# Three-pass scores from split keys, a bias kept in DRAM and half sums on GpSimd, in a two-layer cross-attention kernel

## The chip, the cores and the metric

The kernel runs on one core of a Trainium2 chip. The metric is device time in microseconds. A core has TensorE (PE; its weight loads are listed apart as PEld), VectorE (DVE), ScalarE (ACT), GpSimd (POOL) and SyncE (SP, which here only issues transfers). Each engine runs its own instructions in order; they wait for each other by semaphores. SBUF is the on-chip memory, PSUM the banks in which matrix products are added up.

## The reference

64 batches of 128 queries x 128 channels go through two layers. Each layer is a gated cross-attention with 16 heads of 64 over 77 keys (context rows of 128 channels), and a gated feed-forward part, on normalised x:

```
q, k, v = x @ Wq, context @ Wk, context @ Wv          # 16 heads of 64
sim  = einsum('bhid,bhjd->bhij', q, k) * 64 ** -0.5   # layer 1: masked keys get -max
attn = softmax(sim, axis=-1)
out  = einsum('bhij,bhjd->bhid', attn, v) -> (B, N, 1024) @ Wo + bo
x    = x + tanh(g) * out
```

The feed-forward part of layer 0 is a quantised GELU one, that of layer 1 a spiking one with five steps. The change leaves both alone.

## The kernel before

**Stages.** fold_weights (layer 0), attention (0), quantised_ffn, fold_weights (1), attention (1), spiking_ffn. Folding makes, per head, A = Wk^T Wq and B = Wv Wo as 128 x 128 matrices, and keeps each as a high half in f32r and a low half (`Ahi`, `Alo`, `Bhi`, `Blo`). So a head's "keys" are A times the context, and scores are one product of turned x with them.

**Attention.** 64 slots, one for each batch t, with a 65th to finish. Four batches are a group (b = t % 4 is the slot in its group), eight an octet. In slot t:
- keys for the next group: four heads a slot. A product is three f32r passes of 128 x 308 (hi.hi, lo.hi, hi.lo; make_keys, L512 to L514) into one of two PSUM banks pP; ScalarE copies it out (L656) to G, an f32 tile with two sides, one a group.
- values for the next octet: `PLAN` = 3,3,3,3,3,3,2,0 a slot, three passes of 512 columns (L523 to L525) into the same two banks; ScalarE copies them to a ring ST (L662), SyncE sends them to DRAM, and fetches them back a batch at a time (send, fetch).
- scores of batch t: three full-precision f32 products (`UNITS`: 6, 6 and 4 heads; L573) of XT and G into banks pS0 to pS2. VectorE takes row maxima (L810) and subtracts them into E (L820); ScalarE does the exponential in place (L696); VectorE sums over the 77 keys (L854) and takes the reciprocal (L856); GpSimd multiplies in three parts (L898) into PN.
- batch t-1: TensorE turns PN in ten chunks (turn_probs, L593), ScalarE copies them (L705), TensorE multiplies with the fetched values (weigh, L608) into pO; VectorE adds the result to x (residual, L829) in slot t+1 of the program.
- once a group, for later ones: statistics (b=0, L744 to L752), normalise (b=1, L758), turn_x and its copy (b=2, L506, L652), statistics_after (b=2, L766 to L778; in layer 0 also row maxima and minima L769, L770), context turning and splitting (b=3, L99 to L113), and in layer 1 mask_bias (b=3, L738).

**Order.** It is written out by hand in each engine's `slot`. On TensorE: produce 0, 1, scores 0, produce 2, scores 1, (turn x or context), produce 3, scores 2, produce 4, turn_probs 0, produce 5, turn_probs 1, produce 6, weigh 0, turn_probs 2, weigh 1, weigh 2; keys and values alternate in `produce`. A product waits until ScalarE has copied out the one two before it. On VectorE: maximum 0, residual, shift 0, maximum and shift 1, (context low half), maximum and shift 2, then statistics, normalise, statistics_after or mask_bias, and last the sum and reciprocal.

**Mask, layer 1.** x is widened by a constant channel, so row 127 of G holds a bias per key. SyncE loads 308 mask bytes a group (load_mask, L439), VectorE makes 0 or -2^100 of them (mask_bias), and SyncE places that in four transfers (place_mask, L462). In slot b=3 mask_bias(group+2) waits for a load that SyncE issues at the top of its next slot, behind fetch(t+1).

## Time and profile before

Median of three runs 1606.85 us (1605.63 to 1610.71). The profiled execution took 1606.41 us, its span (first to last instruction) is 1604.8 us.

| | whole span | 300 to 400 us (layer 0) | 1000 to 1100 us (layer 1) |
|---|---|---|---|
| TensorE busy | 90% | 99.4 us | 95.3 us |
| VectorE busy | 68% | 69.9 | 62.5 |
| ScalarE busy | 56% | 65.0 | 60.6 |
| GpSimd busy | 39% | 37.5 | 38.2 |
| granted TensorE clock, of 2.4 GHz | 0.97 | 1.00 | 0.97 |
| DMA share | 36% | 46% | 43% |

A busy time is a share of a stretch, and the ends of matrix products in the records are modelled and overlap the next one's start; what one costs in a full stream is the step from its start to the next. Where an engine was idle ahead of an instruction, the timeline gives the idle time and the engine and line that ended it. "SPq" is SyncE's queue. The slots of the first attention end at about 624 us, those of the second run from about 837 to 1442 us.

### The profile page before, as it was taken

The numbers are of one execution on the slowest core, as the hardware profiler recorded it, in microseconds if no ns is written. First come the engines' busy times: TensorE is split into PE (matmuls) and PEld (weight loads), VectorE is DVE, ScalarE is ACT, GpSimd is POOL, SyncE is SP. The second block draws the span as 40 slices with busy tenths as digits, with TensorE's granted clock in tenths as the row PEclk, the third lists the DMA queues.
The fourth block names the chain that finished last, engine by engine and source line by source line (L and its number), as shares of the span: only waits on it lengthen the run. The fifth ranks groups of instructions, "written<-read, shape, count | busy, mean of one in ns | idle before, by whom it ended". The sixth has DMA issues, their size and how long they took to land. (4 is left out here: it accounts for less than half of the span.)

```text
span 1604.8 us, 27395 instructions
## 1 busy us (share of the span) xinstructions
PE 1447.1 (90%) x9094; PEld 1200.3 (75%) x9094; DVE 1089.5 (68%) x2356; ACT 903.2 (56%) x1903; POOL 624.0 (39%) x747
## 2 busy tenths in 40 slices
PE   6999999999999986559798999898999999977996
PEld 5888888888888874229777878787878787766884
DVE  5676676776777776898655757575656665773886
ACT  3666666666666653660155656565656565545662
POOL 1233434334334333840113333333334342445885
PEclk9999999999999999899999999999999999998998
DMA  8554444444444422100064444444444444320111
GB/s 253 178 157 134 141 153 131 159 130 154 136 151 130 146 80 69 30 0 0 18 192 136 131 139 132 131 130 133 133 135 133 134 128 134 100 64 1 33 33 40
DMA packets 198330, 182.27 MB, mean 114 GB/s; under 512 B 14145, under 2 KB 195393, under 8 KB 198209
## 3 DMA queue, kind: packets, MB, share of 16 engines
q1 hardware_dynamic: 197632, 180.60, 35.8%
q8 instruction: 67, 1.10, 0.3%
q14 instruction: 55, 0.44, 0.1%
q10 hardware_dynamic: 576, 0.13, 0.0%
HBM read 95.43 MB, written 84.93 MB: 112 GB/s over the span
## 5 line engine op out<-in xcount | busy, mean ns | idle before, releaser
L898 POOL TENSOR_TENSOR PN<-E,RC 128x512 f32<-128x512 f32 (+1 forms) x384 | 336.7, 906 | 584.7 <-DVE RC L856 583.7
L810 DVE TENSOR_REDUCE MX<-pS 128x6 f32<-128x462 f32 (+1 forms) x384 | 222.2, 579 | 260.2 <-PE pS L573 260.2
L608 PE MATMUL pO<-work,PT 128*128 128x128 f32 (+1 forms) x2560 | 331.7, 277 | 29.1 <-ACT PT L705 29.1
L656 ACT ACTIVATE G<-pP 128x308 f32<-128x308 f32 (+1 forms) x488 | 209.0, 429 | 244.3 <-PE pP L514 244.1
L608 PEld LDWEIGHTS pO<-work,PT 128*128 128x128 f32 (+1 forms) x2560 | 309.4, 192 | 37.3 <-issue 35.4
L573 PE MATMUL pS<-G,XT 128*128 128x462 f32 (+1 forms) x768 | 324.4, 507 | 0.0
L696 ACT ACTIVATE E<-E 128x462 f32<-128x462 f32 (+1 forms) x384 | 209.6, 546 | 152.5 <-DVE E L820 144.6
L512 PE MATMUL pP<-Chi,Ahi 128*128 128x308 f32 x496 | 240.5, 485 | 1.4 <-ACT G L656 1.2
L820 DVE TENSOR_TENSOR E<-pS,MX 128x462 f32<-128x462 f32 (+1 forms) x384 | 223.7, 582 | 9.1 <-issue 0.2
L705 ACT ACTIVATE PT<-pT 128x512 f32<-128x512 f32 (+1 forms) x384 | 201.0, 523 | 49.7 <-PE pT L593 49.7
L593 PE MATMUL pT<-ident,PN 128*128 128x128 f32 (+1 forms) x1280 | 202.6, 277 | 27.5 <-POOL PN L898 27.5
L854 DVE TENSOR_REDUCE SM<-E 128x16 f32<-128x1232 f32 x128 | 183.4, 1432 | 34.6 <-ACT E L696 34.1
L662 ACT ACTIVATE ST<-pP 128x512 f32<-128x512 f32 x290 | 172.1, 594 | 46.7 <-PE pP L525 41.5
L593 PEld LDWEIGHTS pT<-ident,PN 128*128 128x128 f32 (+1 forms) x1280 | 159.0, 141 | 48.9 <-issue 31.9
L523 PE MATMUL pP<-Bhi,Vhi 128*128 128x512 f32 x300 | 153.6, 512 | 12.1 <-PEq L145 9.3
L573 PEld LDWEIGHTS pS<-G,XT 128*128 128x128 f32 x768 | 136.2, 188 | 24.1 <-issue 6.4
L513 PE MATMUL pP<-Chi,Alo 128*128 128x308 f32 x496 | 151.3, 305 | 0.0
L514 PE MATMUL pP<-Clo,Ahi 128*128 128x308 f32 x496 | 151.1, 305 | 0.0
L512 PEld LDWEIGHTS pP<-Chi,Ahi 128*128 128x128 f32 x496 | 95.1, 192 | 35.3 <-issue 20.8
L524 PE MATMUL pP<-Blo,Vhi 128*128 128x512 f32 x300 | 121.0, 403 | 0.0
L525 PE MATMUL pP<-Bhi,Vlo 128*128 128x512 f32 x300 | 120.9, 403 | 0.0
L513 PEld LDWEIGHTS pP<-Chi,Alo 128*128 128x128 f32 x496 | 95.1, 192 | 32.2 <-issue 25.3
(194 smaller groups left out, 1960.3 us busy)
## 6 DMA issues: line engine op xcount, KB each, us to landing
values<-ST SPq DMA_DIRECT2D x256, 256.0 KB
work<-values SPq DMA_DIRECT2D x512, 128.0 KB
values<-ST SPq DMA_DIRECT2D x64, 208.0 KB
work<-values SPq DMA_DIRECT2D x128, 104.0 KB
C<-in_ctx SPq DMA_DIRECT2D x32, 154.0 KB
out<-s_O SPq DMA_DIRECT2D x16, 256.0 KB, 2.3
work<-in_L_xattn_Wq SPq DMA_DIRECT2D x2, 512.0 KB, 7.4
work<-in_L_xattn_Wkv SPq DMA_DIRECT2D x2, 512.0 KB, 7.8
```

What stands on the lines that cost most here:

```text
L512: nc.tensor.matmul(out, p["Ahi"][:, head, :], hi, start=True, stop=False)
L513: nc.tensor.matmul(out, p["Alo"][:, head, :], hi, start=False, stop=False)
L573: nc.tensor.matmul(out, XT[:, half, b, :], G[:, half, b, h0:h1, :].rearrange("p h k -> p (h k)"), start=True, stop=True).then_inc(score_re ...
L593: last = nc.tensor.transpose(pT[n % 2][0:rows, c - c0, :], PN[(t - 1) % 2][:, start:start + rows], p["ident"][:, :])
L608: last = nc.tensor.matmul(pO[:, 0:CH], PT[0:rows, c, :], V[(t - 1) % VRING][0:rows, tile, CH * hh:CH * hh + CH], start=c == 0, stop=c == C ...
L656: return nc.scalar.activation(G[0:live, g % 2, :, head, :], bank[0:live, 0:KEYCOLS].rearrange("p (b k) -> p b k", k=KEYS), ACT.Copy)
L696: nc.scalar.activation(e, e, ACT.Exp).then_inc(exp_done, 1)
L705: nc.scalar.activation(PT[0:rows, c0:c1, :], pT[n % 2][0:rows, 0:c1 - c0, :], ACT.Copy).then_inc(p_out, 1)
L810: nc.vector.tensor_reduce(MX[:, h0:h1], pS[u][:, 0:(h1 - h0) * KEYS].rearrange("p (h k) -> p h k", k=KEYS), X_AXIS, ALU.max).then_inc(max_ ...
L820: nc.vector.tensor_tensor(E[t % 2][:, h0:h1, :], pS[u][:, 0:(h1 - h0) * KEYS].rearrange("p (h k) -> p h k", k=KEYS), MX[:, h0:h1].unsqueez ...
L854: nc.vector.tensor_reduce(SM[:, :], E[t % 2][:, :, :], X_AXIS, ALU.add).then_inc(sum_done, 1)
L898: nc.gpsimd.tensor_tensor(out, e, scale, ALU.mult).then_inc(prob_ready, 1)
```

## The change

- Scores: x and keys are both kept as high and low f32r halves, and a score product is three passes of 308 columns (x_hi.k_hi, x_hi.k_lo, x_lo.k_hi), four of them a slot (`UNITS` is now four units of 4 heads), in three banks that are used in turn.
- Keys: instead of G with two sides there are Ghi and Glo with one 4 x 4 grid of cells each. Slot b of a group uses up a row of cells and refills it with the next group's keys; the next group reads them the other way round. A keys product is now copied out twice: ScalarE writes the high half, then VectorE the low half (`keys_lo`), and the bank is free after that.
- Order: values stand ahead of keys. VectorE does residual, statistics, normalise and statistics_after ahead of the first maximum, and the four low halves at the slot's end, with the total between the third and the fourth.
- Sum: E gets a 78th column of zeros; GpSimd adds columns 0 to 38 to columns 39 to 77 (into PN, which is free then), and VectorE reduces 16 x 39 instead of 16 x 77.
- Mask: in fold_weights of layer 1 all 64 x 77 mask bytes are loaded and turned into a bias, four heads wide, which goes to DRAM. In attention SyncE places a row of four cells a slot from there. The mask_bias of each group is gone. GpSimd zeroes Glo's last rows at the start.
- sem_clear moves from the second attention to the quantised feed-forward part.

```
-UNITS = [(0, 6), (6, 12), (12, 16)]
+UNITS = [(4 * u, 4 * u + 4) for u in range(4)]
+SCORES = len(UNITS)
+HALF = KEYPAD // 2
...
-            out = []
-            for j in range(4):
-                out += keys[j:j + 1] + values[j:j + 1]
-            return out
+            return values + keys
...
+        def cell(tile, g, b, quarter):
+            return tile[:, b, quarter, :] if g % 2 == 0 else tile[:, quarter, b, :]
...
# SyncE, slot t, between the sends and fetch(t + 1)
+                if layer == 1 and group + 1 < GROUPS:
+                    sp.wait_ge(score_ready, SCORES * (t + 1))
+                    place_bias(group + 1, t % GROUP)
...
# TensorE, produce
                         wait(pe, made_out, m - 1)
+                        if m >= 2 and KINDS[m - 2] == "key":
+                            pe.wait_ge(lo_out, keys_to(m - 1))
...
# TensorE, scores
+                    wait(pe, shifted, n - 2)
+                    out = pS[n % 3][:, 0:4 * KEYS]
+                    hi, lo = cell(Ghi, group, b, u), cell(Glo, group, b, u)
+                    nc.tensor.matmul(out, XThi[:, half, b, :], hi, start=True, stop=False)
+                    nc.tensor.matmul(out, XThi[:, half, b, :], lo, start=False, stop=False)
+                    nc.tensor.matmul(out, XTlo[:, half, b, :], hi, start=False, stop=True).then_inc(score_ready, 1)
...
# TensorE, order of slot t (v values, K0 to K3 keys): S0 V0 S1 V1 (turn) S2 V2 S3 K0
#   turn_probs0 K1 turn_probs1 K2 weigh0 turn_probs2 K3 weigh1 weigh2; with no values K0 is ahead of S3
...
# ScalarE, produced
                         if kind == "key":
-                            keys_out(pP[m % 2], group + 1, which).then_inc(made_out, 1)
+                            act.wait_ge(score_ready, SCORES * (t + 1))
+                            keys_hi(pP[m % 2], group + 1, which).then_inc(made_out, 1)
...
# ScalarE, order: V0 exp0 V1 (x_hi or context_hi) exp1 V2 K0 exp2 probs0 K1 exp3 probs1 K2 probs2 K3
...
# VectorE
+                def low(j):
+                    if values + j < len(todo):
+                        m = MADE[t] + values + j
+                        dve.wait_ge(made_out, m + 1)
+                        keys_lo(pP[m % 2], group + 1, todo[values + j][1]).then_inc(lo_out, 1)
+
+                def total():
+                    if cur:
+                        dve.wait_ge(half_done, t + 1)
+                        nc.vector.tensor_reduce(SM[:, :], PN[t % 2][:, 0:HEADS * HALF].rearrange("p (h k) -> p h k", k=HALF),
+                                                X_AXIS, ALU.add).then_inc(sum_done, 1)
...
                 if t >= 2:
                     residual(t - 2)
...
                 if b == 2 and t >= GROUP and cur:
                     dve.wait_ge(x_done, group * GROUP)
                     statistics_after(group - 1)
+                row_max(0)
+                shift(0)
+                row_max(1)
+                shift(1)
+                if b == 2 and nxt:
+                    x_lo(group + 1)
...
+                row_max(2)
+                shift(2)
+                row_max(3)
+                shift(3)
+                low(0)
+                low(1)
+                low(2)
+                total()
+                low(3)
...
# GpSimd
+            def halves(t):
+                pool.wait_ge(exp_done, SCORES * (t + 1))
+                wait(pool, p_turned, (t - 1) * 3)
+                nc.gpsimd.tensor_tensor(PN[t % 2][:, 0:HEADS * HALF].rearrange("p (h k) -> p h k", k=HALF),
+                                        E[t % 2][:, :, 0:HALF], E[t % 2][:, :, HALF:KEYPAD], ALU.add).then_inc(half_done, 1)
```

## Rows read from the trace of the kernel before

**Rows 1.** Timeline of TensorE, layer 0: start us, us, engine, line, operation, tiles.
```profile
303.99 0.60 PE L593 MATMUL pT<-ident,PN 128*128 128x128 f32 x4
...
304.71 0.30 PE L514 MATMUL pP<-Clo,Ahi 128*128 128x308 f32 x1
304.86 1.05 PE L608 MATMUL pO<-work,PT 128*128 128x128 f32 x8
305.75 0.38 PE L593 MATMUL pT<-ident,PN 128*104 128x128 f32 x2
...
307.45 0.30 PE L513 MATMUL pP<-Chi,Alo 128*128 128x308 f32 x1
...
308.20 0.39 PE L525 MATMUL pP<-Bhi,Vlo 128*128 128x512 f32 x1
308.43 0.94 PE L573 MATMUL pS<-G,XT 128*128 128x462 f32 x2
...
309.34 0.30 PE L513 MATMUL pP<-Chi,Alo 128*128 128x308 f32 x1
```

**Rows 2.** Timeline of VectorE: reciprocals of slots 30, 54, 58; 74 and 114 (layer 1).
```profile
335.42 0.25 DVE L856 RECIPROCAL RC<-SM 128x16 f32<-128x16 f32 x1
...
554.66 0.25 DVE L856 RECIPROCAL RC<-SM 128x16 f32<-128x16 f32 x1
...
588.03 0.25 DVE L856 RECIPROCAL RC<-SM 128x16 f32<-128x16 f32 x1
...
933.17 0.25 DVE L856 RECIPROCAL RC<-SM 128x16 f32<-128x16 f32 x1
...
1329.30 0.25 DVE L856 RECIPROCAL RC<-SM 128x16 f32<-128x16 f32 x1
```

**Rows 3.** Timeline of VectorE, layer 0: slots with b=0 (309 us) and b=2 (328 us).
```profile
309.40 0.64 DVE L810 TENSOR_REDUCE MX<-pS 128x6 f32<-128x462 f32 x1 [2.51 <-PE pS L573]
...
312.88 0.86 DVE L744 BATCH_NORM_STATS2 BN<-X 128x6 f32<-128x128 f32 x4
...
314.36 1.44 DVE L854 TENSOR_REDUCE SM<-E 128x16 f32<-128x1232 f32 x1
...
328.30 0.34 DVE L829 SCALAR_TENSOR_TENSOR X<-pO,gate,X 128x128 f32<-128x128 f32 x1
328.55 0.63 DVE L820 TENSOR_TENSOR E<-pS,MX 128x462 f32<-128x462 f32 x1
...
330.60 0.48 DVE L810 TENSOR_REDUCE MX<-pS 128x4 f32<-128x308 f32 x1 [0.20 <-PE pS L573]
331.12 0.48 DVE L820 TENSOR_TENSOR E<-pS,MX 128x308 f32<-128x308 f32 x1
331.51 0.86 DVE L766 BATCH_NORM_STATS2 BN<-X 128x6 f32<-128x128 f32 x4
...
333.95 1.43 DVE L854 TENSOR_REDUCE SM<-E 128x16 f32<-128x1232 f32 x1
```

**Rows 4.** Timeline of TensorE and VectorE, start of attention 1 and its slots 18 to 20.
```profile
811.29 0.50 PE L523 MATMUL pS<-Bhi,Vhi 128*128 128x512 f32 x1 [2.27 <-ACT ST L662]
...
1008.50 0.86 DVE L766 BATCH_NORM_STATS2 BN<-X 128x6 f32<-128x128 f32 x4
...
1010.13 1.44 DVE L854 TENSOR_REDUCE SM<-E 128x16 f32<-128x1232 f32 x1
...
1027.43 0.31 DVE L738 TENSOR_SCALAR MB<-M 1x308 f32<-1x308 uint8 x1 [9.12 <-DMA M<-in_mask_BxS_bf]
...
1030.67 1.09 PE L593 MATMUL pT<-ident,PN 128*128 128x128 f32 x4 [4.01 <-POOL PN L898]
```

**Rows 5.** Groups by line and form: xcount, busy us, mean ns of one, idle time before.
```profile
L898 POOL TENSOR_TENSOR PN<-E,RC 128x512 f32<-128x512 f32 x256 | 271.4, 1082 | 584.7 <-DVE RC L856 583.7 <-PE pT L593 1.0
...
L883 POOL TENSOR_TENSOR X<-X,gbias 128x512 f32<-128x512 f32 x32 | 40.8, 1275 | 2.5 <-DVE XN L758 2.5
L652 ACT ACTIVATE XT<-pO 128x512 f32<-128x512 f32 x32 | 18.6, 581 | 0.6 <-PE pO L506 0.5
```

More of the change, by code:

```diff
@@ L178, in _ @@
                 load_weights(sp, p, w, loaded)
+            if layer == 1:
+                sp.dma_start(M8[:, :], w["mask"].rearrange("o (b k) -> (o b) k", k=KEYS)).then_inc(m_in, 16)
             sp.wait_ge(padded, CTX)
@@ L316, in _ @@
             if layer == 1:
+                dve.wait_ge(m_in, 16)
+                nc.vector.tensor_scalar(MB[:, :, :], M8[:, :].unsqueeze(1).to_broadcast([BATCH, 4, KEYS]), MASKED, -MASKED,
+                                        ALU.mult, ALU.add).then_inc(bias_made, 1)
                 dve.wait_ge(loaded["q"], 16)
@@ L348, in tile_rows, with attention @@
     return 128 if t < TILES - 1 else PAIR * TAIL
-def attention(nc, p, layer, ctx, ctx_dram, mask_dram):
+def attention(nc, p, layer, ctx, ctx_dram):
     with ExitStack() as s:
@@ L421, in products @@
             values = [("value", start + j) for j in range(PLAN[n])] if octet < OCTETS else []
-            out = []
-            for j in range(4):
-                out += keys[j:j + 1] + values[j:j + 1]
-            return out
+            return values + keys
+        KINDS = [kind for t in range(BATCH) for kind, _ in products(t)]
         MADE = [0]
@@ L612, in weigh @@
                         last.then_inc(out_ready, 1)
-                produce(0)
-                produce(1)
+                values = sum(1 for kind, _ in todo if kind == "value")
                 scores(0)
-                produce(2)
+                if values > 0:
+                    produce(0)
                 scores(1)
+                if values > 1:
+                    produce(1)
                 if b == 2 and nxt:
@@ L625, in slot @@
                     turn_context(nc, p, ctx, pO, group + CTX)
-                produce(3)
                 scores(2)
-                produce(4)
+                if values > 2:
+                    produce(2)
+                if values == 0:
+                    produce(0)
+                scores(3)
+                if values > 0:
+                    produce(values)
                 turn_probs(0)
-                produce(5)
+                produce(values + 1)
                 turn_probs(1)
-                produce(6)
+                produce(values + 2)
                 if prev:
                     if b == 2 and nxt:
-                        pe.wait_ge(xt_out, group + 2)
+                        pe.wait_ge(xhi_out, group + 2)
+                        pe.wait_ge(xlo_out, group + 2)
                     if b == 3 and cur and group + CTX < GROUPS:
@@ L640, in slot @@
                 turn_probs(2)
+                produce(values + 3)
                 weigh(1)
@@ L706, in probs_out @@
                                              ACT.Copy).then_inc(p_out, 1)
-                produced(0)
-                produced(1)
-                produced(2)
+                values = sum(1 for kind, _ in todo if kind == "value")
+                if values > 0:
+                    produced(0)
                 exps(0)
+                if values > 1:
+                    produced(1)
                 if b == 2 and nxt:
-                    x_out(group + 1)
+                    x_hi(group + 1)
                 if b == 3 and cur and group + CTX < GROUPS:
@@ L804, in slot @@
                 nxt = cur and group + 1 < GROUPS
+                todo = products(t) if cur else []
+                values = sum(1 for kind, _ in todo if kind == "value")
                 def row_max(u):
@@ L849, in slot @@
                     statistics_after(group - 1)
-                if b == 3 and cur and layer == 1 and group + 2 < GROUPS:
-                    mask_bias(group + 2)
-                if cur:
-                    dve.wait_ge(exp_done, (t + 1) * 3)
-                    nc.vector.tensor_reduce(SM[:, :], E[t % 2][:, :, :], X_AXIS, ALU.add).then_inc(sum_done, 1)
-                    dve.wait_ge(sum_done, t + 1)
-                    nc.vector.reciprocal(RC[:, t % 2, :], SM[:, :]).then_inc(recip_done, 1)
-                else:
+                row_max(0)
[4 more added lines that the diff above has]
+                    x_lo(group + 1)
+                if b == 3 and cur and group + CTX < GROUPS:
+                    dve.wait_ge(chi_out, group + CTX + 1)
+                    context_lo(nc, ctx, pO, group + CTX)
+                row_max(2)
[7 more added lines that the diff above has]
+                low(3)
+                if not cur:
                     residual(BATCH - 1)
@@ L919, in _ @@
                     tile_context(nc, pool, ctx, group + CTX)
+                halves(t)
                 pool.wait_ge(recip_done, t + 1)
-                wait(pool, p_turned, (t - 1) * 3)
                 for n in range(3):
@@ L1008, in _ @@
             def _(pool):
+                nc.gpsimd.sem_clear(range(min(p["spent"]), max(p["spent"]) + 1))
                 pool.wait_ge(step, 3)
@@ L1623, in folded @@
                 fold_weights(nc, p, layer, w[layer], loaded[layer], ctx, a["ctx_1024"], ffn)
-                attention(nc, p, layer, ctx, a["ctx_1024"], mask)
+                attention(nc, p, layer, ctx, a["ctx_1024"])
         spiking = {"W_fc": a["L1_ffn_W_fc"], "W_proj": a["L1_ffn_W_proj"], "gate": a["g_ffn"][1:2],
```

215 lines of the change are left out of this document (106 added, 109 removed).

## The prediction

> **What bounds the kernel now.** I read the busy table and the stretches first (the numbers are in the table ahead of the diff): in the first attention TensorE is busy 99 of 100 us, VectorE 70, ScalarE 65, GpSimd 38. So there the end is set by TensorE, and I priced its slot from the starts in its timeline. (Ends are modelled; the step from one start to the next is what an instruction costs.) A pass of a keys product (f32r, 308 columns) steps 0.145 us, a pass of a values product (512) 0.23. Four transposes cost 0.43 (303.99 to 304.71, less two key passes), four products of weigh 0.89, the last two transposes and six products 1.555. A full-precision score product of 462 columns costs 0.765 (308.43 to 309.34 less a pass), so 1232 columns cost 2.04 [rows 1]. With three values a slot is 2.04 + 4 x 0.435 + 3 x 0.69 + 0.86 + 0.89 + 1.555 = 9.16. Eight slots with 20 values hold 70.5, and 1.5 more for four turns of x and context: 72.0. The reciprocals of slots 30 and 54 stand 219.2 apart, 73.1 an octet [rows 2]: the sum explains the slot to 1.5%.
>
> The second attention has the same work but 79.2 us an octet [rows 2]. There the mask lands late. VectorE sits idle 9.12 us for it in slot 3 of an octet, GpSimd gets its reciprocals late, TensorE idles 4.01 us, and its four transposes behind the gap take 1.09 us where [rows 1] has 0.60: the clock is at 1.2 instead of 2.4 GHz [rows 4]. So a late mask costs 6.1 us an octet, 4.0 of gap and 2.1 of clock.
>
> **What the change takes away.** (1) Scores: twelve f32r passes of 308 columns, 12 x 0.145 = 1.74, for 2.04: 0.30 less of TensorE in a slot, 38 us in 128 slots if TensorE stays the bound. No row shows this pass with scores; it has the keys' shape and type. The other end is 1.2 times as long, which would leave nothing. I take 0.145. (2) The mask: it is made once and placed from DRAM by four transfers a group. The last is issued in slot 3 behind its S3 and the values' sends and is needed by S3 of the next slot, some 6 us later. VectorE's wait in [rows 4] is long because the load is issued only after a fetch that waits for the slot's end; nothing of that kind stands ahead of the new transfers. I take the stall as gone, bounds 0 and the whole 6.1 an octet; if a fetch queued behind it were late, weigh would wait, but that is a slot further on. (3) The sum over keys on VectorE: 1.47 to the reciprocal (333.95 to 335.42) [rows 2, 3] becomes about half, 0.83.
>
> **What it adds to VectorE.** Four lows in a slot (PSUM and SBUF in, 308 elements, as the shift of this shape: step 0.39, 0.48 until done) [rows 3]: 1.56. Four maxima and shifts instead of three: (0.51 + 0.39) x 4 = 3.60. Residual 0.25. With the total and reciprocal 1.0 this is 6.4 a slot; statistics add 1.48 in a group's slot b=0, normalising about 1.0 in b=1 (four steps like the residual's), the after-statistics 2.44 in b=2 (1.63 in the second attention), and x_lo 0.6 [rows 3, 4]. VectorE holds 63 us an octet: not the bound by itself.
>
> **Where the path goes: the new wait.** TensorE may make K2 only when VectorE has done low(0), because both use one pP bank. And low(0) stands in VectorE's order behind the whole slot: residual(t-2), then the group's extra work X, four maxima and shifts. The residual itself waits for the end of TensorE's previous slot, and the extra work, formerly at the slot's tail under other work, now stands ahead of the first maximum. So the two engines alternate. Count from TensorE's S0: its work is seen by VectorE 0.2 later (S starts at 308.43, costs 0.77, its maximum starts at 309.40) [rows 1, 3]; residual 0.25; X; 3.60; low(0) 0.47; 0.14 back to TensorE (estimate: GpSimd follows VectorE and TensorE follows GpSimd by 0.1 to 0.2). K2 starts no sooner than 4.67 + X. TensorE itself gets there after S 1.74, three V 2.07, K0 and K1 0.87, two transposes 0.86: 5.54. Behind K2 stand K2, weigh(0), K3 and the rest, 0.435 + 0.89 + 0.435 + 1.555 = 3.315. Hence a slot:
> b=0: X 1.48, K2 at 6.15, slot 9.47. b=1: X 1.0, K2 at 5.67, slot 9.0.
> b=2, first attention: X 2.44. Here x_lo also waits for ScalarE, which does exp(0), V1 and x_hi after the first shift: x_hi 0.58 [rows 5], V1 the same size at a step 0.1 shorter, exp(0) about 0.35 by its 308 of 512 elements: shift(0) is done at 3.9, x_hi at 5.3, x_lo to 5.95, two maxima and shifts 1.8, low(0) and the way back 0.61: K2 at 8.35, slot 11.67. Second attention, X 1.63: 10.9.
> b=3: no X; maxima wait for the scores, and context turning and its low add: K2 at about 6.05, slot 9.4. Without values (slot 7) TensorE is there at 3.8 but low(0) is done only at 5.2: 8.55.
> An octet: 2 x (9.47 + 9.0 + 11.67) + 9.4 + 8.55 = 78.2 in the first, 76.7 in the second attention.
>
> The adding of halves on GpSimd (624 outputs) lies between the last exponential and the total. Nearest rows: 1.08 and 1.28 for 512 [rows 5], so 1.3 to 1.55; I take 1.35, nearer to the multiply, which also reads E. In b=0 the exponentials end at 6.4, halves 7.75, total and reciprocal 8.8, low(3) 9.3, the next residual 9.67: hidden, with 0.3 to 0.4 of cover, and beyond it each slot pays in full. The cover for the probabilities is larger: they are needed 4 us into the next slot. ScalarE's exponentials grow by one instruction, hidden.
>
> A rule of the Trainium skill speaks against the placing: the page SBUF — State Buffer, section Who interferes with whom, says that VectorE and GpSimd share one pair of ports and that a VectorE instruction in a 2-port mode (tensor_scalar from SBUF can be one) blocks for the whole of a GpSimd instruction. Nothing in the rows shows these two at once; it is the fourth rival below.
>
> **The sum**, against the profiled execution (1606.4 us, of it 1604.8 span; the median of the runs is 1606.85, so no correction):
> first attention, seven octets x (78.2 - 73.1) = +36;
> second, seven x (76.7 - 79.2) = -17;
> the end of each: slots 55 to 58 have no values and took 33.4 [rows 2]; they become 8.55 + 9.47 + 9.0 + 11.2 = 38.2, +5 each, +10;
> starts: the lows of the first 16 heads add about 1 each; folding now waits for a mask load before centring (+2, bounds 1 and 3); eight placing transfers ahead of the first sends become four (0 to -5). I take 0, bounds -4 and +5;
> clock: TensorE now waits about 2.2 us at a stretch in the b=2 slots of the first attention and in half of the second's, 21 in all. One gap of 2.27 was followed by a first values pass of 0.50 [rows 4] (0.39 is usual), and the 4.01 gap by 1.2 GHz. Between none and all 21 at 2.1 each (0 to +44) I take a third, +15, as the gap row nearest is a doubtful case.
> 1606.4 + 36 - 17 + 10 + 0 + 15 = 1650; I give 1648.
>
> **Rivals.**
> 1. Every long wait in b=2 drops the clock: 31 x 2.1 = 65 instead of 15: 1698. For: the 2.27 row. Against: the first attention's granted clock is 1.00 throughout, though with no such gaps.
> 2. Halves much slower, 2.2 us: some 0.5 beyond the cover in 128 slots, +64: 1712. It decides from 1.7 us on. Against: both rows of 512 elements stay under 1.3.
> 3. The alternation is shorter than worked, by 0.5 us a slot: then b=0 9.0, b=1 8.9, b=2 11.2, b=3 9.2, slot 7 8.05: octets of 75.4 and 73.8, +16 and -38, ends +6, hardly a clock drop, 1589: faster. It decides from about 0.3 us a slot; such a gain needs VectorE's steps to overlap more than in [rows 3], which are back to back already. For: the total rests on ten small latencies.
> 4. The shared ports: in b=1 normalising starts while GpSimd still multiplies for the slot before (its reciprocal comes at 8.9 of a 9.5 us slot). A wait for one multiply, 1.1, in 31 slots: +34, 1682.
> 5. VectorE's order does not bind and TensorE stays the bound: octets 73.1 - 2.4 and the mask stall gone, 7 x 2.4 + 7 x 8.5 = 76 and 5 at the ends: 1525. For: 30% of VectorE's time is idle today. Against: K2's wait is in the text of the kernel. (If the f32r pass is no faster, this is 1563.)
> 6. Errors cancel: the mask's 43 us and the scores pay for the new waits: within 0.3%, which is about what a measurement of this kernel can tell from no change.
>
> **Chances.** Forecast 0.56 (own range 1615 to 1672), rival 1 0.08, 2 0.05, 3 0.12, 4 0.05, 5 0.06, 6 0.08. Slower: 0.56 + 0.08 + 0.05 + 0.05 = 0.74; same 0.08; faster 0.18. The range 1588 to 1692 takes in the forecast, 4, 6, most of 3 and the lower part of 1, about 0.8.
>
> **What would show it.** In the trace after: TensorE's keys product waiting for a VectorE low in each slot, about 2 us where b=2, 0.1 to 0.6 elsewhere; reciprocals 78 and 77 us an octet apart; the 4.01 us wait of the transposes in the second attention gone; score passes stepping 0.145; halves 1.35; the first maximum after the statistics, 3 us behind the slot's start in b=2. Wrong if VectorE shows idle time before low(0) in b=0 and b=1 slots, if halves end after low(2) by over 0.5, or if the granted clock leaves 1.0 in the first attention.

## The result, and the profile after

The changed kernel takes 1732.26 us (median of four runs, 1729.44 to 1734.2), the kernel before 1607.49 in the same comparison: a ratio of 1.077, 95% interval 1.0757 to 1.0786. It is slower by 7.7%. The forecast was 1648 with a range up to 1692: the sign was right, the size was off by 84 us, and the range did not hold the time.

The busy line of the page after, then two stretches (us of busy time in 100, then granted clock and DMA share), then reciprocals of VectorE: one octet in the first attention, slots 54 and 58 at its end, one octet in the second attention.

```profile
PE 1478.8 (85%) x9846; PEld 1311.5 (76%) x9862; DVE 1339.2 (77%) x3129; ACT 913.7 (53%) x2047; POOL 817.6 (47%) x876
```
```profile
300.00:400.00 100.00, 88.89 (x601) 80.11 (x602) 80.38 (x204) 56.09 (x133) 46.52 (x51) 0.98 0.38 121
...
1000.00:1100.00 100.00, 91.81 (x620) 83.06 (x620) 80.51 (x209) 56.73 (x135) 50.85 (x55) 0.98 0.42 131
```
```profile
238.74 0.25 DVE L876 RECIPROCAL RC<-SM 128x16 f32<-128x16 f32 x1
...
324.07 0.25 DVE L876 RECIPROCAL RC<-SM 128x16 f32<-128x16 f32 x1
...
633.99 0.25 DVE L876 RECIPROCAL RC<-SM 128x16 f32<-128x16 f32 x1
...
675.83 0.25 DVE L876 RECIPROCAL RC<-SM 128x16 f32<-128x16 f32 x1
...
1023.54 0.25 DVE L876 RECIPROCAL RC<-SM 128x16 f32<-128x16 f32 x1
...
1105.57 0.25 DVE L876 RECIPROCAL RC<-SM 128x16 f32<-128x16 f32 x1
```

TensorE falls from 99.4 to 88.9 busy us in 100 and nobody takes its place: VectorE reaches 80. That fits two engines that take turns. An octet of the first attention takes 85.3 us (324.07 - 238.74), where [rows 2] had 73.1 and the forecast 78.2; one of the second 82.0 for 79.2 and a forecast 76.7; four slots of the first's end 41.8 for 33.4 and a forecast 38.2. From first to last reciprocal the first attention grew from 563.5 to 658.7 us (+95) and the second from 605.3 to 637.4 (+32); the head, what lies between and the tail changed by under 2 us each. So the loss is all inside the slots.

TensorE of the changed kernel, first attention. The L593 rows of 356.13, 366.58 and 324.43, 337.05 are the starts of slots (b=1, b=2; b=2, b=3); the L527 rows are K2.

```profile
324.43 0.39 PE L593 MATMUL pS<-Ghi,XThi 128*128 128x308 f32 x1
...
333.75 0.39 PE L527 MATMUL pP<-Chi,Ahi 128*128 128x308 f32 x1 [1.03 <-ACT Ghi L686]
...
337.05 0.39 PE L593 MATMUL pS<-Ghi,XThi 128*128 128x308 f32 x1
337.28 0.30 PE L594 MATMUL pS<-Glo,XThi 128*128 128x308 f32 x1
337.42 0.30 PE L595 MATMUL pS<-Ghi,XTlo 128*128 128x308 f32 x1
337.56 0.39 PE L538 MATMUL pP<-Bhi,Vhi 128*128 128x512 f32 x1
...
356.13 0.39 PE L593 MATMUL pS<-Ghi,XThi 128*128 128x308 f32 x1
...
363.30 0.38 PE L527 MATMUL pP<-Chi,Ahi 128*128 128x308 f32 x1 [0.17 <-DVE Glo L820]
...
366.58 0.39 PE L593 MATMUL pS<-Ghi,XThi 128*128 128x308 f32 x1
...
375.91 0.38 PE L527 MATMUL pP<-Chi,Ahi 128*128 128x308 f32 x1 [2.03 <-ACT Ghi L686]
376.41 1.76 PE L629 MATMUL pO<-work,PT 128*128 128x128 f32 x8
```

VectorE of the changed kernel in the same stretch (and one row of a b=0 slot ahead of it), and what GpSimd does beside it.

```profile
306.04 0.49 DVE L777 TENSOR_SCALAR VE<-MV 128x4 f32<-128x4 f32 x1
...
327.34 0.93 DVE L801 COPY mv<-MV 128x8 f32<-128x8 f32 x1
328.19 0.46 DVE L848 TENSOR_REDUCE MX<-pS 128x4 f32<-128x308 f32 x1
...
333.14 0.99 DVE L820 TENSOR_TENSOR Glo<-pP,Ghi 128x308 fp32r<-128x308 f32 x2
...
356.42 0.35 DVE L882 SCALAR_TENSOR_TENSOR X<-pO,gate,X 128x128 f32<-128x128 f32 x1
356.68 2.42 DVE L783 TENSOR_SCALAR XN<-X,MV,RS 128x128 f32<-128x128 f32 x4
359.03 0.46 DVE L848 TENSOR_REDUCE MX<-pS 128x4 f32<-128x308 f32 x1
...
362.68 0.47 DVE L820 TENSOR_TENSOR Glo<-pP,Ghi 128x308 fp32r<-128x308 f32 x1
```
```profile
326.95 1.29 POOL L935 TENSOR_TENSOR X<-X,gbias 128x512 f32<-128x512 f32 x1
...
356.16 2.60 POOL L957 TENSOR_TENSOR PN<-E,RC 128x512 f32<-128x512 f32 x3 [1.20 <-DVE RC L876]
```

Three things stand here. First, K2 starts 0.15 and 0.14 after low 0 is done (362.68 + 0.47 = 363.15, K2 at 363.30; 333.14 + 0.47 = 333.61, K2 at 333.75). The row at 333.75 names ScalarE's copy (L686), but in the code K2 asks only for K0's copy and K0's low half, and K0's copy was done at 331.85; where an engine named by a row had long been done, another of the awaited semaphores was last. From K2 to the next slot are 3.28 and 3.30 us, 3.315 in the forecast. Second, the four normalises of b=1 take 2.42 and end 0.34 after GpSimd's three multiplies (356.16 + 2.60 = 358.76); in the kernel before the normalises stood at the slot's tail, like the statistics of [rows 3], clear of the multiplies. Third, the copy of eight numbers for a row (mv) takes 0.93 and ends with GpSimd's adding of the bias (326.95 + 1.29 = 328.24).

Groups by line and form of the changed kernel (count, busy us, mean ns of one, idle before), and one group of the kernel before.

```profile
L942 POOL TENSOR_TENSOR PN<-E 128x624 f32<-128x624 f32 x128 | 194.4, 1519 | 486.4 <-ACT E L723 486.4
...
L873 DVE TENSOR_REDUCE SM<-PN 128x16 f32<-128x624 f32 x128 | 102.8, 803 | 48.8 <-POOL PN L942 48.7
...
L783 DVE TENSOR_SCALAR XN<-X,MV,RS 128x128 f32<-128x128 f32 x64 | 37.5, 645 | 1.1 <-POOL RS L929 1.1
...
L801 DVE COPY mv<-MV 128x8 f32<-128x8 f32 x32 | 17.7, 554 | 1.1
```
```profile
L758 DVE TENSOR_SCALAR XN<-X,MV,RS 128x128 f32<-128x128 f32 x64 | 17.8, 342 | 1.1 <-POOL RS L877 1.1
```

### The profile page after: what moved, and what is told of

It is laid out like the page before. It is cut to its first block and busy times, and to the rows that moved or that the text cites. A ratio compares the mean times of both kernels' runs of the same rounds, so it can differ in the third digit from the quotient of the medians.

```text
span 1732.4 us, 31024 instructions
## 1 busy us (share of the span) xinstructions
PE 1478.8 (85%) x9846; PEld 1311.5 (76%) x9862; DVE 1339.2 (77%) x3129; ACT 913.7 (53%) x2047; POOL 817.6 (47%) x876
## 5 line engine op out<-in xcount | busy, mean ns | idle before, releaser
L942 POOL TENSOR_TENSOR PN<-E 128x624 f32<-128x624 f32 x128 | 194.4, 1519 | 486.4 <-ACT E L723 486.4
L723 ACT ACTIVATE E<-E 128x308 f32<-128x308 f32 x512 | 236.3, 462 | 282.8 <-DVE E L859 280.4
L820 DVE TENSOR_TENSOR Glo<-pP,Ghi 128x308 fp32r<-128x308 f32 (+1 forms) x496 | 229.3, 463 | 125.9 <-ACT Ghi L686 123.4
L527 PE MATMUL pP<-Chi,Ahi 128*128 128x308 f32 x496 | 192.9, 389 | 98.9 <-ACT Ghi L686 72.1
L859 DVE TENSOR_TENSOR E<-pS,MX 128x308 f32<-128x308 f32 x512 | 244.9, 478 | 27.2 <-DVE MX L848 1.4
L848 DVE TENSOR_REDUCE MX<-pS 128x4 f32<-128x308 f32 x512 | 240.0, 469 | 4.2
L686 ACT ACTIVATE Ghi<-pP 128x308 fp32r<-128x308 f32 (+1 forms) x496 | 213.9, 432 | 17.3 <-PE pP L529 12.8
L593 PE MATMUL pS<-Ghi,XThi 128*128 128x308 f32 x512 | 179.1, 350 | 47.4 <-DVE E L859 45.3
L527 PEld LDWEIGHTS pP<-Chi,Ahi 128*128 128x128 f32 x496 | 96.0, 193 | 143.2 <-ACT Ghi L686 83.0
L593 PEld LDWEIGHTS pS<-Ghi,XThi 128*128 128x128 f32 x512 | 96.8, 189 | 82.3 <-DVE E L859 61.3
L594 PE MATMUL pS<-Glo,XThi 128*128 128x308 f32 x512 | 155.6, 304 | 0.0
L595 PE MATMUL pS<-Ghi,XTlo 128*128 128x308 f32 x512 | 155.6, 304 | 0.0
L873 DVE TENSOR_REDUCE SM<-PN 128x16 f32<-128x624 f32 x128 | 102.8, 803 | 48.8 <-POOL PN L942 48.7
```

Of the source, the lines that this page charges most:

```text
L527: nc.tensor.matmul(out, p["Ahi"][:, head, :], hi, start=True, stop=False)
L593: nc.tensor.matmul(out, XThi[:, half, b, :], hi, start=True, stop=False)
L686: return nc.scalar.activation(head_rows(Ghi, g, head), by_key(bank[0:live, :], KEYS), ACT.Copy)
L723: nc.scalar.activation(e, e, ACT.Exp).then_inc(exp_done, 1)
L820: return nc.vector.tensor_tensor(head_rows(Glo, g, head), by_key(bank[0:live, :], KEYS), head_rows(Ghi, g, head).bitcast(F32), ALU.subtract)
L848: nc.vector.tensor_reduce(MX[:, h0:h1], pS[n % 3][:, 0:(h1 - h0) * KEYS].rearrange("p (h k) -> p h k", k=KEYS), X_AXIS, ALU.max).then_inc( ...
```

## The experiments

All are compared with the kernel before on the same chip, whose median was 1607.2 to 1607.6 each time. Ratios are to it. After the result I had two theories of the surplus over 1648. **Port**: VectorE's tensor_scalar and copy wait out GpSimd's instructions. **Order**: whatever stands ahead of maximum 0 delays exponential 0, and with it everything in ScalarE's and VectorE's fixed orders, up to low 0 and K2. A further question was what the low halves, the halves on GpSimd and the mask are each worth.

### The normalise alone moved back

```
-                if b == 1 and nxt:
-                    normalise(group + 1)        # ahead of row_max(0)
...
                 shift(2)
+                if b == 1 and nxt:
+                    normalise(group + 1)
                 row_max(3)
```

> The changed kernel with one edit: in a group's second slot VectorE normalises x between shift 2 and maximum 3 instead of ahead of maximum 0. Same work, still ahead of the first low half, but at a time when GpSimd is idle. Theory (VectorE's normalising is held up by GpSimd's multiplies of the slot before): four steps fall from 2.4 us to 1.1, the slot from 10.45 to about 9.1, 31 slots, 1732 - 42 = 1690. Rival (normalising costs 2.4 us wherever it stands, or something else sets these slots): the group of four stays at 2.4 us and the time at 1732.

1683.72 us, 1.0466 (1.0448 to 1.0483): 48.5 less than the changed kernel. The normalise is back at its old price:

```profile
L783 DVE TENSOR_SCALAR XN<-X,MV,RS 128x128 f32<-128x128 f32 x64 | 17.7, 340 | 1.1 <-POOL RS L929 1.1
```

The port theory stands for these slots: they went from 10.45 to 9.69, and all b=1 slots together gave back 27 us. That is less than expected (9.1 a slot, 42 us in all). At its new place the normalise stands behind maxima that wait for their scores (they start 1.12 apart, as the scores do), so its 1.11 us still delay low 0. The total came out near the expectation because another 19 us came from the b=2 slots, mostly through the clock: weighings of over 1.4 us (1.05 is usual) fell from 13 to 7. That part was luck.

### All extra work behind the lows

Now the statistics of b=0 and b=2 too go behind shift 3, between low 1 and low 2, and GpSimd makes the inverse deviation behind its halves.

```
-                if b == 0 and nxt:
-                    statistics(group + 1)
-                if b == 2 and t >= GROUP and cur:
-                    dve.wait_ge(x_done, group * GROUP)
-                    statistics_after(group - 1)
                 row_max(0)
...
                 low(0)
                 low(1)
+                if b == 0 and nxt:
+                    statistics(group + 1)
+                if b == 2 and t >= GROUP and cur:
+                    dve.wait_ge(x_done, group * GROUP)
+                    statistics_after(group - 1)
                 low(2)
                 total()
                 low(3)
...
# GpSimd
-                if b == 0 and nxt:
-                    inverse_deviation(group + 1)
...
                 halves(t)
+                if b == 0 and nxt:
+                    inverse_deviation(group + 1)
```

> e1_norm_mid, and statistics (b=0) and after-statistics (b=2) moved from ahead of maximum 0 to between the low halves 1 and 2; GpSimd takes the inverse deviation after the halves. Theory (TensorE's third keys product waits for a low half that stands behind this work, so it lies on the path): octets fall from 85.3 and 82.0 us to about 74.5 and 73.6, 1732 - 144 = 1588, bounds 1575 to 1610. Rival (the lows, maxima and halves alone set the slot, the extra work was covered): not below 1670.

1607.69 us, 0.9998 (0.9987 to 1.001): a further 76 less, equal to the kernel before. The place of the extra work (with GpSimd's one step that goes with it) is worth 124.6 us of the changed kernel, as much as its whole loss against the kernel before. The 76 lie in the b=2 slots (64 less) and in those of b=0 (25 less); those of b=3 in the first attention grew by 7. Some of it is clock: one weighing in all is over 1.4 us now.

### The mask alone, in the kernel before

The kernel before loads all masks once, in place of a load a group behind a fetch that waits for the slot's end.

```
-                sp.dma_start(M8[0:1, g % 2, :], mask_dram[0:1, g * KEYCOLS:(g + 1) * KEYCOLS]).then_inc(m_in[g % 2], 16)
+                sp.dma_start(M8[0:1, :], mask_dram[0:1, :]).then_inc(m_in[0], 16)
...
-                if layer == 1 and t % GROUP == 0 and 1 <= group < GROUPS - 1:
-                    sp.wait_ge(bias_ready, group)
-                    load_mask(group + 1)
...
-                dve.wait_ge(m_in[g % 2], 16 * (g // 2 + 1))
+                dve.wait_ge(m_in[0], 16)
```

> The kernel before with one edit: all 64 x 77 mask bytes are loaded once at the start of the second attention, the four placing transfers stay. Theory (a late mask costs a 4.0 us gap and 2.1 us of clock an octet): octets of the second attention fall from 79.2 to 73.1 us, 1607 - 43 = 1564. Rival (the stall covers other waits that come up in its place, so the mask was cheap): 1595 or more.

1562.89 us, 0.9718 (0.9702 to 0.9734), as expected: the wait of [rows 4] costs 44.6 us. The octets of the second attention take 73.2, and its stretch from first to last reciprocal falls from 605.3 to 563.7. The changed kernel should have this gain too, so that its other parts cost about 125 + 45 = 170 us: without its low halves and in a late order (the run of 1528 us below) its two attentions take the same time, 544.9 and 545.3, with no mask stall left.

### No halves on GpSimd

VectorE sums the 16 x 77 of E itself.

```
-                        dve.wait_ge(half_done, t + 1)
-                        nc.vector.tensor_reduce(SM[:, :], PN[t % 2][:, 0:HEADS * HALF]...
+                        dve.wait_ge(exp_done, SCORES * (t + 1))
+                        nc.vector.tensor_reduce(SM[:, :], E[t % 2][:, :, 0:KEYS],
...
-                halves(t)
```

> The changed kernel without the halves on GpSimd: VectorE sums 16 x 77 of E itself. Theory (VectorE's own order decides, the next residual waits for low 3 behind the total): 1.47 for 0.84 us on VectorE less 0.3 of waiting for GpSimd, about 0.3 a slot slower, 1732 + 40 = 1770. Rival (the add on GpSimd is a step on the path that costs more than it saves): 1732 - 40 = 1690.

1727.67 us, 1.0738 (1.072 to 1.0756): neither of the two figures, and a sum of two effects that cancel. The total of VectorE takes 80 us more over the run (182.5 for 102.8) and waits 45 less, and the slots of b=1 grow from 10.46 to 10.67, those of b=2 without a clock drop from 12.62 to 12.84. Against that, weighings of over 1.4 us fell from 13 to 7, and the b=2 slots are 8.5 us shorter in sum. So GpSimd's help does shorten slots here; the few us the other way are the clock's.

### The weighing ahead of K2

```
                 turn_probs(1)
-                produce(values + 2)
                 (waits of the turns)
                 weigh(0)
+                produce(values + 2)
                 turn_probs(2)
```

> The changed kernel with one edit on TensorE: weigh(0), 0.89 us that need no low half, runs ahead of the third keys product instead of behind it. Theory A (one loop: TensorE's end of slot, residual, extra work, maxima, low 0, third keys product): 0.5 to 0.9 us less in each slot, 1732 - 96 = 1636. Theory B (a second loop lies 0.1 us under the first: residual, extra work, maxima, last exponential, halves 1.52, total 1.0, low 3, next residual, 7.9 us plus the extra work): little is gained, 1732 - 25 = 1707.

1721.44 us, 1.0715 (1.0696 to 1.0735). Only 11 us, and not where theory A has them: the slots of b=0 and b=1 grew (9.51 to 9.85, 10.46 to 10.69; 10 us in all), those of b=3 shrank by 5. The gain is in the b=2 slots of the second attention, 13 us, where every other one had taken 12.55 and none does now (10.97). So TensorE's work behind K2 does not set the ordinary slot. That VectorE's list does is the likelier reading; this run alone does not show it.

> e5_w0_first with both loops cut: VectorE sums 16 x 77 of E itself (no halves on GpSimd), and low 3 runs ahead of the total. Theory B: now the gain of the first loop appears, 6.9 us an octet, 1732 - 100 = 1632. If the halves are not what caps e5, this is no faster than e5.

This run has both edits above and low 3 ahead of the total. It took 1848.18 us, 1.1489, and was my worst miss. VectorE at a slot's end:

```profile
360.50 0.99 DVE L820 TENSOR_TENSOR Glo<-pP,Ghi 128x308 fp32r<-128x308 f32 x2
362.86 0.48 DVE L820 TENSOR_TENSOR Glo<-pP,Ghi 128x308 fp32r<-128x308 f32 x1 [1.37 <-ACT Ghi L686]
...
363.91 1.42 DVE L873 TENSOR_REDUCE SM<-E 128x16 f32<-128x1232 f32 x1
365.37 0.25 DVE L876 RECIPROCAL RC<-SM 128x16 f32<-128x16 f32 x1
```

VectorE stands idle 1.37 us for the copy of K2, and low 3, the total of 1.42, the reciprocal and the whole next slot queue behind that wait. The run with the weighing alone in front has such waits too. Over the whole run the lows' waits grew from 193 us there to 230 here, and the total's busy time from 102 to 183: 118 together, beside 127 us between the two runs.

### The same edits with the extras at the tail

> e2_extras_tail (1607.7 us; normalising inside, statistics behind low 1) with weigh(0) ahead of the third keys product. Theory B: part of the 0.5 to 1.6 us that TensorE waits in a slot there goes, the halves loop caps it: 1585, bounds 1565 to 1600. Theory A: 1540.

1586.75 us, 0.9876 (0.986 to 0.9893), as expected: 21 less than with K2 first. With nothing ahead of maximum 0 the weighing's place does count.

> e7_tail_w0 without the halves and with low 3 ahead of the total. Theory B: octets of about 72.5 us, near TensorE's sum of 70.6: 1545, below the 1563 of e3_before_mask. If VectorE's load (63 + 5 us an octet, with its waits) binds instead: about 1590.

1628.73 us, 1.014 (1.0122 to 1.0158), 42 us more. The total of VectorE takes 81 us more over the run, and half of it shows. But this run also has low 3 ahead of the total, and no run takes the halves alone out of this order; how the 42 us divide stays open. The b=2 and b=3 slots carry 35 of them.

> e7_tail_w0 (1586.8 us) with VectorE's tail reordered: low 0, low 1, total over 16 x 77 of E (no halves), statistics or after-statistics, low 2, low 3. In e6 and e8 low 2 and low 3 sat idle 1.4 us for ScalarE and the total stood behind them, so the next residual came late. Theory (VectorE's order, from residual to residual, is the loop; its idle time ahead of low 2 can hold the total): octets of 73.5 us instead of 75.7, 1554. If the work on VectorE alone binds (68.5 us an octet and its idle time), no better than 1586.

VectorE sums 16 x 77 ahead of the extras, behind low 1. 1643.02 us, 1.0224 (1.0207 to 1.0241): a miss, too. VectorE rises to 88.4 busy us in 100, low 3 slides into the next slot, and TensorE's first values product there waits for it:

```profile
318.89 0.47 PE L538 MATMUL pP<-Bhi,Vhi 128*128 128x512 f32 x1 [1.57 <-DVE Glo L820]
```

### The changed kernel without the keys' low halves

```
-                        if m >= 2 and KINDS[m - 2] == "key":
-                            pe.wait_ge(lo_out, keys_to(m - 1))
...
-                        wait(pe, lo_out, HEADS * (group - 1) + 4 * (u + 1))
+                        wait(pe, made_out, MADE[t])
...
-                low(0)
-                low(1)
-                low(2)
                 total()
-                low(3)
```

> The changed kernel with the low halves of keys left out in the slots (only the first group's are made, later scores read old ones): 1.56 us less of VectorE a slot, and TensorE's keys products wait only for ScalarE's copy. Order, halves, three passes stay. Theory (the bank's release by VectorE's low half is what puts the whole order of VectorE on TensorE's path): octets of about 74, 1580. Rival (order and halves alone cost it, through shifts and scores): 1680 or more.

1664.62 us, 1.0353 (1.0317 to 1.0388), between the two. The b=1 slots still take 10.41 (10.45 with the lows), and the row that does it is there unchanged:

```profile
299.64 2.77 DVE L781 TENSOR_SCALAR XN<-X,MV,RS 128x128 f32<-128x128 f32 x4
...
303.42 0.46 ACT L721 ACTIVATE E<-E 128x308 f32<-128x308 f32 x1 [2.32 <-DVE E L857]
303.44 0.41 PE L591 MATMUL pS<-Ghi,XThi 128*128 128x308 f32 x1 [0.72 <-DVE E L857]
...
304.42 0.41 PE L527 MATMUL pP<-Chi,Ahi 128*128 128x308 f32 x1 [0.29 <-ACT ST L689]
```

Mostly b=2 got shorter, in the first attention from between 12.6 and 14.2 down to 11.1. So low 0 and K2's wait are not the only way from maximum 0 to TensorE. Two others bind in b=1: S3 needs the bank that shift 0 frees (it waits 0.72), and K0 needs a copy that ScalarE makes behind exponential 0 (0.29).

### The new order alone, in the kernel before

```
-                row_max(0)
                 if t >= 2:
                     residual(t - 2)
+                if b == 0 and nxt:
+                    statistics(group + 1)
+                if b == 1 and nxt:
+                    normalise(group + 1)
+                if b == 2 and t >= GROUP and cur:
+                    dve.wait_ge(x_done, group * GROUP)
+                    statistics_after(group - 1)
+                row_max(0)
```

> The kernel before with the changed kernel's order of VectorE's extra work alone: residual, statistics, normalise and after-statistics ahead of maximum 0. Theory (there no product waits for VectorE, so its place costs only what ScalarE's first exponential delays, in b=2): 1610, at most 1625. Rival (the order costs by itself, as in the changed kernel): 1660 or more.

1671.24 us, 1.0392 (1.0374 to 1.0409). The rival was right: with no low half, no new wait and no new scores the order costs 64 us. From first to last reciprocal the first attention grew by 27 us and the second by 39. In the second the mask's stall still stands, and five weighings there take over 1.4 us where the kernel before has one; the order was not run in a kernel without that stall, so 27 is the clean part. One slot with b=2 of the first attention shows how (VectorE, ScalarE and TensorE merged by time):

```profile
339.56 0.91 DVE L776 COPY mv<-MV 128x8 f32<-128x8 f32 x1
...
340.39 0.62 DVE L810 TENSOR_REDUCE MX<-pS 128x6 f32<-128x462 f32 x1
...
341.79 0.59 ACT L696 ACTIVATE E<-E 128x462 f32<-128x462 f32 x1 [2.11 <-DVE E L820]
...
343.41 0.41 PE L512 MATMUL pP<-Chi,Ahi 128*128 128x308 f32 x1 [0.91 <-ACT ST L662]
...
344.78 1.13 PE L608 MATMUL pO<-work,PT 128*128 128x128 f32 x8 [0.24 <-ACT PT L705]
```

ScalarE is idle 2.11 us for the first shift, and behind its exponential stand, in order, the copy of x^T and the values' copy for which TensorE then waits 0.91, and the probabilities' copy for which it waits 0.24.

> The kernel before with the residual ahead of maximum 0 in every slot and, in b1, the normalise behind it; statistics and statistics after stay behind shift 2. In the run with the whole new order the b1 slots were 0.4 us longer and the stretch from b2 to b3 0.95 and 1.27. So the theory (the statistics of b2 carry it) expects here two b1 slots an octet x 0.4 x 16 octets = 13 us: 1620, at most 1632. Rival (the port held by GpSimd's multiplies, four normalises at 0.60 for 0.34, is most of the 64): 1645 or more.

> The kernel before with the residual ahead of maximum 0 in every slot and, behind it, the statistics of b0 and the statistics after of b2; the normalise stays behind shift 2. Theory (the statistics of b2 carry it: exponential 0 of b2 comes late and ScalarE's copies of keys and values, in order behind it, hold TensorE): 64 - 13 = 51 us, 1650 to 1665. Rival (the port carries it): 1625 or less.

The normalise alone: 1622.33 us, 1.0083 (1.0059 to 1.0108), +15. The statistics alone: 1658.49 us, 1.0309 (1.0268 to 1.035), +51. Both came out as forecast, and together they make 66, near the 64 of the whole order; the residual stands ahead of maximum 0 in both, and what that alone costs was not run. In the kernel before the statistics carry the cost (how much of it is the copy of mv, at 578 ns for 172, was not separated), although the normalises in their run took 606 ns where 342 is usual: a delay of one engine costs only what its followers have no slack for.

### What is left when nothing waits for the lows

> The changed kernel in the order of the extras-last run with the weighing ahead of K2, and without the keys' low halves in the slots (TensorE waits only for ScalarE's copy and the scores read the low halves of the first group: part of the work left out). Theory: the low halves are all that is left between 1587 and a TensorE-bound kernel; without them it runs at the masks-once kernel's 1563 less 0.30 us a slot for the cheaper scores (128 x 0.30 = 38 us): 1525, within 15. Rival: four maxima and shifts, the halves and x_lo hold it as well: 1560 or more, and 0.4 us a slot is theirs.

1574.8 us, 0.9797 (0.9771 to 0.9823): by the numbers the rival, by its trace neither. As in the run without the lows above, part of the work is left out. Ordinary slots take 9.18 to 9.21 and TensorE shows a hole of its own, which I had made by moving K2 away. The second turn and the weighing, from the run with the low halves and the weighing first (TensorE, ScalarE, TensorE):

```profile
319.00 0.60 PE L614 MATMUL pT<-ident,PN 128*128 128x128 f32 x4
319.01 0.59 ACT L732 ACTIVATE PT<-pT 128x512 f32<-128x512 f32 x1
...
319.74 1.13 PE L629 MATMUL pO<-work,PT 128*128 128x128 f32 x8
```

Four transposes step 0.36 when another instruction follows (341.65 to 342.01 in the changed kernel), so TensorE is free at 319.36 and starts the weighing at 319.74. The row shows no wait, since the modelled end of the transposes, 319.60, covers most of it. Two runs separate that hole from VectorE's load:

> The extras-last kernel (K2 ahead of the weighing, as in the changed kernel), without the keys' low halves in the slots (the later groups read the low halves of the first: part of the work left out). Theory: the 50 us by which the run with the weighing first lay above its TensorE-bound 1525 are that idle 0.38 us a slot, which K2 fills where nothing waits for low halves: 1525 to 1535. Rival: the maxima, shifts, halves and x_lo hold it: 1570 or more.

> The extras-last kernel with the weighing ahead of K2, and ScalarE copies the first turned probabilities (PT, 0.59 us) ahead of exponential 2 in place of behind it. With the weighing ahead of K2 TensorE has nothing between the second turn and the weighing: the turn ends at 319.36, PT's copy ends at 319.60 and the weighing starts at 319.74, 0.38 us idle in the ordinary slots, the same in the run without the low halves, whose slots are 9.18 to 9.21. Theory: with the copy 0.35 us earlier this goes, 0.3 to 0.38 x 127 = 38 to 48 us: 1540 to 1550. Rival: exponentials 2 and 3 come 0.6 later, the halves and the total with them, and the next slot's VectorE chain gives it back: 1575 to 1600.

Without the lows (they are left out here too) and with K2 back in the hole: 1528.14 us, 0.9502 (0.9484 to 0.952), where 1525 was worked out for a kernel bound by TensorE.

```profile
312.27 0.39 PE L527 MATMUL pP<-Chi,Ahi 128*128 128x308 f32 x1
...
312.78 1.05 PE L627 MATMUL pO<-work,PT 128*128 128x128 f32 x8
```
```profile
300.00:400.00 100.00, 98.38 (x721) 93.41 (x720) 74.95 (x205) 67.43 (x159) 56.32 (x64) 1.00 0.47 148
```

With the lows, the weighing first and only this edit on ScalarE

```
-                exps(2)
                 probs_out(0)
+                exps(2)
```

the kernel takes 1558.11 us, 0.9687 (0.9669 to 0.9705): 29 less than without it, short of the 38 to 48 expected. Of 0.38 us in front of the weighing 0.15 is left:

```profile
313.75 0.60 ACT L732 ACTIVATE PT<-pT 128x512 f32<-128x512 f32 x1
...
313.98 0.60 PE L614 MATMUL pT<-ident,PN 128*128 128x128 f32 x4
...
314.49 1.13 PE L629 MATMUL pO<-work,PT 128*128 128x128 f32 x8
```

Nothing is left out here, and it is the fastest such version of the study, though only 5 us ahead of the kernel before with its masks loaded once.

### The sum of the runs

| step | us | difference |
|---|---|---|
| kernel before | 1607.5 | |
| masks loaded once | 1562.9 | -44.6 |
| the changed kernel's other parts (f32r scores in four units, halves, mask placing), extra work late, lows left out | 1528.1 | -34.8 |
| with the keys' low halves | 1607.7 | +79.6 |
| statistics ahead of maximum 0 | 1683.7 | +76.0 |
| normalise ahead of maximum 0 (the changed kernel) | 1732.3 | +48.6 |

The differences are those of this sequence; each holds the clock drops that its step brings or takes away.

## Why the prediction was right or wrong

**The mechanism that was worked out is there; two of its terms were mis-sized, and two other roads were missing.** TensorE takes turns with VectorE through low 0 and K2. The slots that need neither tensor_scalar nor ScalarE in their chain came out as worked: b=0 9.51 (346.62 to 356.13; 9.47 forecast; 9.77 behind slot 7), b=3 9.57 (9.4), 3.28 behind K2 (3.315). In b=0 too a small tensor_scalar takes 0.49 (306.04), where its group in the kernel before has 0.17: the same thing that went wrong in b=1, but small.

**X in b=1 was the first term mis-sized.** "Normalising about 1.0 in b=1" took 2.35 (356.68 to 359.03). With it K2 comes 7.17 behind the slot's start instead of 5.67, and the slot takes 10.45 instead of 9.0: 1.45 twice an octet, 2.9. This is the mechanism of rival 4, to which I gave 0.05, and which I priced at one multiply (1.1) in 31 slots, 34 us. Moving the normalise back gave 48.5, of which 27 came in the b=1 slots and 19 in those of b=2, mostly clock. The Trainium skill, SBUF — State Buffer, section Who interferes with whom, says that the engine that comes second is blocked while the other's whole instruction lasts. The trace agrees: the 2.42 us of normalises end 0.34 behind the three multiplies, and the copy ends with the bias. What I did not draw from the rule is that four normalises can meet three multiplies in a row, not one, and that small tensor_scalars and copies fall under it as well.

**X in b=2, the second, was short by the same cause**: mv at 0.93 instead of 0.17 (its next instruction starts 0.85 behind it, where the sum had about 0.1) brings the first maximum 3.5 behind the residual's start (324.71 to 328.19). K2 came at 9.32 (333.75 - 324.43) for 8.35, and the slot took 12.62 for 11.67. Where the clock fell behind K2's wait (1.76 for 1.05 at 376.41; granted clock 0.76 of full speed from 375 to 382) it took 14.24 (366.58 to 380.82).

**The octets by these terms**: in the octet that starts with the slot at 324.43, 2 x 1.45 in b=1, 0.95 and 2.57 in the two of b=2, 0.51 in slot 7, 0.51 in the three others: 7.4 over the 78.2, and it took 85.7. By the reciprocals above the surplus was 7.1. In the second attention the b=2 slots came as worked where the clock held (10.95; 10.9 forecast) and at 12.55 in every other one. The surplus in seven octets of 7.1 and seven of 5.3 is 87 us; the two ends add 3.6 and 2.4, together 93, less the 15 already taken for the clock: 1650 + 78 = 1728 for 1734.2 in the profiled execution.

**The clock** cost about what was taken for it, by two errors that cancel. I took a third of 21 waits at 2.1 us, 15. In the changed kernel TensorE waits 2.03 to 2.05 us for K2 in 14 slots, and in 12 of them the slot is 1.6 longer than its like (14.23 for 12.62, 12.55 for 10.95): 19. The row that I called doubtful was not: behind the gap of 2.27 us in the kernel before, the passes from 811.99 to 814.12 take 0.63 each where 0.39 is usual:

```profile
811.99 0.63 PE L525 MATMUL pS<-Bhi,Vlo 128*128 128x512 f32 x1
```

One sign of being wrong that I had named did come, the granted clock in the first attention: 0.98 from 300 to 400 us. The profiled run's mean granted clock is 0.953 for 0.968.

**Confirmed**: the score pass steps 0.14 (337.28, 337.42, 337.56), the first of a run 0.23; the scores in their place were worth 34.8 us with all that goes with them, for 38 forecast; the mask's stall was 44.6, about 6 an octet; rival 5, "VectorE's order does not bind", was worked out at 1525 and came at 1528 once its condition was made true, by a late order and with the lows left out. The lows were given as 1.56 of VectorE and one wait; in the late order they cost 79.6 us.

**Halves** took 1.52 for 1.35; [rows 5] had 1.08 and 1.28 for 512 elements against these 624, so the upper of my two bounds was the right one. VectorE waited 0.31 us for them in ordinary slots. Without them the slots of b=1 and b=2 grew by 0.2, so at 1.52 they still save time; what the 0.17 beyond the forecast cost was not run alone.

**What I had not seen at all** are the other roads from maximum 0 to TensorE. I followed it only to low 0. The order-only run has no low halves and loses 64 us; its rows show the road through ScalarE, whose copies for TensorE stand in order behind exponential 0. S3's wait for shift 0 is a third road. They run beside that over low 0 and hide one another: without the lows the new order costs 1664.6 - 1528.1 = 136.5 us, with them 124.6. So my reason for the loss, the new wait of K2, was true slot by slot and still not the one whose removal would have cured it: without the lows the changed kernel still takes 1664.6. In the first attention, where no mask disturbs, the order costs 27 us in the kernel before and 70 in the changed one (588.2 to 658.7 between first and last reciprocal). Why it is so much more stays partly open; four maxima instead of three and TensorE's shorter scores, which leave less cover, are an argument and were not tried alone.

## What to carry to other kernels

When a change moves work ahead of the first step of an engine's list, follow every consumer of that first step, through each engine's fixed order, not only the one wait that the diff adds. An instruction's duration holds for its place: look at what GpSimd does at the new place, and where VectorE's copies and tensor_scalars meet a run of GpSimd's instructions, price them to the end of that run. Before an instruction is moved for its own wait, ask what its old place covered: K2 hid a copy of 0.6 us, and its removal opened a hole that no row called a wait. And before a small gain or loss is put down to an edit, compare the same slots in both traces: two runs here owed theirs to the clock, while the slots that the edit touched went the other way.

## What the runs showed of the hardware that I had not expected

- A copy of 128 x 8 numbers on VectorE takes 0.17 us alone and 0.93 when GpSimd began a 128 x 512 addition 0.4 us before; a normalise of 128 x 128 takes 0.34 alone, and in the changed kernel, beside multiplies, 0.65 in the mean and up to 1.10. Residual (0.35), maxima (0.47) and statistics (0.86 for four) in the same places keep their time.
- A wait of TensorE of 2.03 to 2.05 us was followed by products at the lower clock, 1.2 GHz, in part at 376 and 546 (1.76 and 1.21 for eight that take 1.05) and at the full clock at 462 (1.05): 12 times of 14 in the changed kernel it cost 1.6 us.
- Clock drops can hide what an edit does to the slots: without GpSimd's halves the ordinary slots of the changed kernel grew by 0.2 us and the run still came out 5 us shorter, with 7 long weighings for 13.
